# Four-layer gated block on one core: score products in adjacent pairs, value product in four column strips

## The chip, the core and the metric

The kernel runs on one NeuronCore of a Trainium2 chip as one launch. The metric is the device time of the launch in microseconds (us). The engines in it are TensorE (PE; its weight loads are listed apart as PEld), VectorE (DVE), ScalarE (ACT), GpSimd (POOL) and the queues that start transfers (SP, POOL).

## The reference

Four residual steps on x (4 batches, 512 tokens, 128 features). The change touches the third one, an attention with 16 heads of 8 features from 512 queries to 77 context rows per batch:

```python
x = x + tanh(g_xattn[0]) * xattn0(ctx, layernorm(x), W_b)            # step A: one head, 77 keys
x = x + tanh(g_ffn[0])   * ffn0(layernorm(x), ...)                    # step B: 8-bit quantised MLP
x = x + tanh(g_xattn[1]) * xattn1(layernorm(x), ctx, ctx, mask, ...)  # step C
x = x + tanh(g_ffn[1])   * moe(layernorm(x), wqkv, w1, w2)            # step D: top 2 of 8 experts

# xattn1
Q = split(query @ W_q.T); K = split(key @ W_k.T); V = split(value @ W_v.T)   # (b, 16, s, 8)
scores = einsum('bhqd,bhkd->bhqk', Q, K) / sqrt(8)
scores = where(mask, -inf, scores)
attn_w = nan_to_num(softmax(scores))
out = einsum('bhqk,bhkd->bhqd', attn_w, V)
return merge(out) @ W_o.T
```

## The kernel before

The program is written with one instruction stream for each engine and semaphores between them; nothing reorders it. Steps A and B come first, then step C with the router of step D woven in, then the scattering of rows to experts, the expert loop over 39 tiles, and the gathering of the result.

**Step C.** A batch b has 4 token tiles of 128 tokens (TB) and 8 score units (UNITS): unit u is token tile u // 2 and half u % 2 of the heads. A head group is four heads (HG), which lie in 32 of the 128 feature rows, and its scores have 4 x 77 = 308 columns (GC). `scores(b, u)` makes two head groups: for each a bf16 product of the identity with the mask values (`mneg`, L629), and on top of it in the same PSUM bank an fp32 product of 32 rows of `qT` with the same 32 rows of `kblk` (L630). On DVE `softmax(b, u)` takes the maximum (L991) and subtracts it (L994); on ACT `expC` takes the exponential (L419) into `pC` (tile name `space`). DVE's `sums` (L1000) adds each head's row. The two halves of `wide` are buffers for units, so unit n waits for the subtraction of unit n - 2.

The 16 heads' 1232 score columns are then cut into key blocks (HCH), here 10 (NCH): nine of 128 columns and one of 80. For each, PE transposes four 128-token pieces (`turn_p`, L651) into bank 2 or 3, ACT copies the result to one of two buffers of `pTC` (`copy_pT`, L427), and PE multiplies with `vblk` (`pv`, L663): `vblk` holds the values of the block's keys, each head's in its own 8 of 128 output columns and zeros elsewhere. All ten products add up in bank 1.

**The order of work in step C.** A hand-written loop of NCH slots n for each batch b sets the order on every engine: PE does `turn_p(b, n)`, `scores(b + 1, n)` while n < 8, and `pv(b, n - 1)`; then come pieces at fixed slots: `turn_r` (L677) and `spread_r` (L682) spread the reciprocals of the row sums in slots 0 and 1, `wo(b - 1)` (L692) is in slot 2, and the router of step D for batch b - 1 has its steps 0, 1, 2 in slots 5, 6, 9. DVE's step 1 of the router is one long run of small instructions (L1033 to L1063); its end releases PE's step 2 (L713, L714). DVE's `softmax(b + 1, 7)` stands behind this run, ACT's `expC(b + 1, 7)` behind that, and ACT's `copy_pT(b, 8)` behind the exponential. `attn_out(b)` (L1016) on DVE ends a batch. Before the first batch's loop, units 2 to 7 of batch 0 run by themselves (unit 0 and 1 a little earlier).

## Time and profile before

| | |
|---|---|
| median of three runs | 472.52 us (469.72 to 472.85) |
| span of the profiled execution, first to last instruction | 471.6 us |
| busy in it: PE, DVE, ACT, POOL | 339.0, 260.9, 140.6, 96.5 us |
| stretch of step C (first score unit to last value product) | 121.3 to 315 us |
| mean granted TensorE clock over the span | 0.764 of full speed |

The profiled execution's time outside its span isn't listed with it; its span lies 0.9 us under the median of the runs and within their spread, so differences in the span are read as differences in the time. Starts are in us from the first instruction. The listed end of a matmul is modelled and overlaps with the next one's start, so a matmul's cost is read from its start to the next one's start.

### The profile page before, as it was taken

What the parts mean: (1) busy time and instruction counts of PE and PEld (TensorE: products, weight loads), DVE (VectorE), ACT (ScalarE), POOL (GpSimd) and SP (SyncE); (2) the same over time, 40 slices, a digit from 0 to 9 for tenths busy, and PEclk for the clock granted to TensorE, in tenths of its full rate; (3) what the DMA queues carried; (4) which work ended last, traced back from release to release, by engine and by line L of the source; (5) the groups of instructions that cost most, each with busy time, mean ns of one, the idle gap of its engine ahead of it and who ended that gap; (6) DMA issues with size and microseconds to landing.
All of it is one profiled execution on the core that took longest, in us unless ns stands there. A gap on an engine that the chain in (4) does not pass through costs nothing.

```text
span 471.6 us, 5266 instructions
## 1 busy us (share of the span) xinstructions
PE 339.0 (72%) x1327; PEld 198.6 (42%) x1329; DVE 260.9 (55%) x753; ACT 140.6 (30%) x310; POOL 96.5 (20%) x156
## 2 busy tenths in 40 slices
PE   1157645545899899999789996862019999999930
PEld 0157521132333434444343553532006777777720
DVE  4748986997336513759862786475702333333314
ACT  1021025452141222333322243311013545455510
POOL 8400000017100000000033002414321334334430
PEclk9999955565555555999955897985557999999975
DMA  8991013900000000000000000101011111111127
GB/s 248 328 330 28 2 8 70 303 0 1 2 0 0 0 1 0 0 1 0 0 18 30 0 0 12 37 11 35 24 47 30 54 44 55 51 52 51 39 58 217
DMA packets 30192, 25.79 MB, mean 55 GB/s; under 512 B 8362, under 2 KB 26273, under 8 KB 30171
## 3 DMA queue, kind: packets, MB, share of 16 engines
q1 hardware_dynamic: 26011, 12.56, 10.2%
q0 software_dynamic: 4160, 12.99, 8.1%
q8 instruction: 9, 0.15, 0.1%
q14 instruction: 12, 0.10, 0.1%
HBM read 11.35 MB, written 14.49 MB: 55 GB/s over the span
## 4 chain that ended last, share of the span: by engine, by line
PE 56%; DVE 26%; issue 7%; DMA 4%; POOL 4%; ACT 2%; SPq 1%; POOLq 0%; DVEq 0%; ACTq 0%
PE wide L630 12%; PE bank L663 7%; PE wide L756 6%; PE bank L771 5%; PE wide L757 5%; PE bank L651 3%; PE wide L629 3%; PE bank L764 3%; DVE st L814 2%; DVE amh L965 2%; DVE h L843 2%; DVE space L961 2%; DMA space<-expert_out 2%; DVE rv L830 1%; POOL expert_rows L339 1%
## 5 line engine op out<-in xcount | busy, mean ns | idle before, releaser
L339 POOL DMA_INDIRECT expert_rows<-pay,slot x32 | 30.8, 964 | 194.8 <-DVE slot L1082 186.3
L630 PE MATMUL wide<-kblk,h2T 32*128 32x308 f32 x128 | 69.5, 633 | 0.0
L663 PE MATMUL bank<-pTC,vblk 128*128 128x512 f32 (+1 forms) x80 | 53.3, 758 | 10.6 <-ACT pTC L427 10.6
L991 DVE TENSOR_REDUCE mC<-wide 128x8 f32<-128x616 f32 x32 | 25.5, 798 | 60.3 <-PE wide L630 60.0
L348 POOL DMA_INDIRECT expert_out<-space x39 | 38.3, 982 | 70.7 <-DVE space L1137 70.7
L1131 DVE TENSOR_TENSOR space<-space,wide 128x352 f32<-128x352 f32 x39 | 20.3, 521 | 58.6 <-PE wide L757 55.9
L419 ACT ACTIVATE space<-space 128x616 f32<-128x616 f32 x32 | 22.8, 716 | 91.3 <-DVE space L994 91.3
L756 PE MATMUL wide<-w_s,space 128*128 x78 | 32.5, 499 | 3.7 <-issue 2.9
L515 PE MATMUL bank<-ident,h 128*128 128x128 f32 x48 | 13.3, 432 | 29.8 <-DVE h L843 29.0
L771 PE MATMUL bank<-w_s,space 128*128 (+1 forms) x234 | 32.8, 276 | 1.0 <-DVE space L1137 1.0
L651 PEld LDWEIGHTS bank<-ident,space 128*128 128x128 f32 (+1 forms) x160 | 23.6, 166 | 22.9 <-issue 18.6
L630 PEld LDWEIGHTS wide<-kblk,h2T 32*128 32x128 f32 x128 | 25.4, 246 | 18.1 <-issue 15.8
L651 PE MATMUL bank<-ident,space 128*128 128x128 f32 (+1 forms) x160 | 29.9, 319 | 2.5 <-ACT space L419 2.5
L757 PE MATMUL wide<-w_s,space 128*128 x78 | 30.7, 476 | 0.0
L771 PEld LDWEIGHTS bank<-w_s,space 128*128 128x128 f32 (+1 forms) x234 | 29.2, 191 | 1.5 <-issue 1.4
L427 ACT ACTIVATE pTC<-bank 128x512 f32<-128x512 f32 (+1 forms) x40 | 23.1, 587 | 20.9 <-PE bank L651 20.9
L476 ACT ACTIVATE space<-wide 128x352 f32<-128x352 f32 x39 | 18.1, 463 | 33.2 <-PE wide L756 33.2
L994 DVE TENSOR_TENSOR space<-wide,mC 128x616 f32<-128x616 f32 x32 | 25.6, 799 | 1.1
L1137 DVE TENSOR_SCALAR space<-bank,space 128x128 f32<-128x128 f32 x39 | 13.7, 351 | 21.9 <-PE bank L771 21.9
L629 PE MATMUL wide<-mneg,identb 128*128 128x308 bf16 x64 | 24.2, 378 | 0.0
L663 PEld LDWEIGHTS bank<-pTC,vblk 128*128 128x128 f32 (+1 forms) x80 | 14.3, 223 | 23.3 <-ACT pTC L427 12.7
L515 PEld LDWEIGHTS bank<-ident,h 128*128 128x128 f32 x48 | 8.6, 217 | 37.0 <-DVE h L843 36.1
(209 smaller groups left out, 512.2 us busy)
## 6 DMA issues: line engine op xcount, KB each, us to landing
expert_rows<-blank POOLq DMA_DIRECT2D x2, 2970.0 KB, 19.2
w_s<-in_w1T SPq DMA_DIRECT2D x1, 2816.0 KB, 10.0
expert_rows<-blank POOLq DMA_DIRECT2D x1, 2574.0 KB, 29.8
space<-expert_rows SPq DMA_DIRECT2D x39, 66.0 KB, 1.8
space<-expert_out SPq DMA_DIRECT2D x8, 256.0 KB, 3.1
xs<-in_x SPq DMA_DIRECT2D x4, 256.0 KB, 5.1
w_s<-in_w2T SPq DMA_DIRECT2D x2, 512.0 KB, 11.9
out<-xs SPq DMA_DIRECT2D x4, 256.0 KB, 3.3
```

The source lines that it names most:

```text
L339: pool.indirect_dma_start(tbl, bass.IndirectOffsetOnAxis(ap=slot[:, k, t:t + 1], axis=0), pay[:, b % 2, k, j, :], None).then_inc(rows_sent ...
L348: pool.indirect_dma_start(planes, bass.IndirectOffsetOnAxis(ap=mpay[:, j, D:D + 1].bitcast(I32), axis=0), my[:, j, :], None, bounds_check= ...
L427: act.activation(pTC[0:w, q % 2, :], bank[2 + q % 2][0:w, :], ACT.Copy).then_inc(pTC_ready, 1)
L629: pe.matmul(o, identb[:], mneg[:, j, None, :].broadcast_to([P, HG, KS]), start=True, stop=False)
L630: ins = pe.matmul(o, qT[r, b, j * P:(j + 1) * P], kblk[r, :, b * KS:(b + 1) * KS], start=False, stop=True)
L651: ins = pe.transpose(bank[2 + q % 2][0:w, j * P:(j + 1) * P], pC[:, (b * TB + j) % (2 * TB), c0:c0 + w], ident[:])
L663: pe.matmul(bank[1][:], vblk[0:w, c, b, :], pTC[0:w, q % 2, :], start=(c == 0), stop=(c == NCH - 1)).then_inc(pv_done, 1)
L756: pe.matmul(wide[:, 2 * p, 0:F], mhT[:, p, :], w1_s[:, bass.ds(e * 2 * F, F)]).then_inc(e_gate, 1)
L757: pe.matmul(wide[:, 2 * p + 1, 0:F], mhT[:, p, :], w1_s[:, bass.ds(e * 2 * F + F, F)]).then_inc(e_w1, 1)
L771: ins = pe.matmul(bank[1][:, p * P:(p + 1) * P], mhidT[0:n, p, c, :], w2_s[0:n, bass.ds(e * NF * D + c * D, D)], start=(c == 0), stop=(c = ...
L991: link(dve.tensor_reduce(m.rearrange("p (g l) -> p g l", g=2), s, AX.X, ALU.max))
L994: dve.tensor_tensor(pC[:, t % (2 * TB), (u % 2) * HU:(u % 2 + 1) * HU].rearrange("p (g l k) -> p g l k", g=2, l=HG), s, m.rearrange("p (g ...
```

## The change

The key blocks follow the head groups: each of the 4 head groups (308 columns) is cut in thirds of 103, 103 and 102 columns, 12 blocks in all, and the block list runs over the four groups first and then over the thirds. A block's keys belong to one head group, so its product fills only 32 output columns. `pv(b, t)` now does the t-th third of all four groups as four products, each to its own 32 partitions of bank 1, from blocks 4t to 4t + 3; it stands in slot 7 (t = 0), in slot 11 (t = 1) and behind the loop (t = 2). `pTC` has 8 buffers, and `vblk` has 32 output columns for a block. `scores` issues both mask products and then both score products. The loop has 12 slots; `sums_end` on DVE moves from slot 9 to slot 11, behind the router's step 2.

```diff
-    HCH = [(c * P, min(P, HK - c * P)) for c in range((HK + P - 1) // P)]
+    THIRD = (GC + 2) // 3
+    HCH = [(g * GC + t * THIRD, min(THIRD, GC - t * THIRD)) for t in range(3) for g in range(NG)]
...
-        va = sb("va", [KS, NB, D]); vblk = sb("vblk", [P, NCH, NB, D])
+        va = sb("va", [KS, NB, D]); vblk = sb("vblk", [P, NCH, NB, HG * DH])
...
-        pTC = sb("pTC", [P, 2, S])
+        pTC = sb("pTC", [P, 2 * NG, S])
...
-                if q >= 2:
-                    act.wait_ge(pv_done, q - 1)
+                if q >= 2 * NG:
+                    act.wait_ge(pv_done, q - 2 * NG + 1)
...
+                o = [wide[:, 2 * (n % 2) + i, 0:GC].rearrange("p (l k) -> p l k", l=HG) for i in range(2)]
                 for i in range(2):
-                    g = 2 * (u % 2) + i
-                    r = slice(32 * g, 32 * g + 32)
-                    o = wide[:, 2 * (n % 2) + i, 0:GC].rearrange("p (l k) -> p l k", l=HG)
-                    pe.matmul(o, identb[:], mneg[:, j, None, :].broadcast_to([P, HG, KS]), start=True, stop=False)
-                    ins = pe.matmul(o, qT[r, b, j * P:(j + 1) * P], kblk[r, :, b * KS:(b + 1) * KS], start=False, stop=True)
+                    pe.matmul(o[i], identb[:], mneg[:, j, None, :].broadcast_to([P, HG, KS]), start=True, stop=False)
+                for i in range(2):
+                    r = slice(32 * (2 * (u % 2) + i), 32 * (2 * (u % 2) + i) + 32)
+                    ins = pe.matmul(o[i], qT[r, b, j * P:(j + 1) * P], kblk[r, :, b * KS:(b + 1) * KS], start=False, stop=True)
                 ins.then_inc(sC_psum, 1)
...
-            def pv(b, c):
-                q, w = NCH * b + c, HCH[c][1]
-                pe.wait_ge(pTC_ready, q + 1)
+            def pv(b, t):
+                q = NCH * b + NG * t
+                pe.wait_ge(pTC_ready, q + NG)
...
-                pe.matmul(bank[1][:], vblk[0:w, c, b, :], pTC[0:w, q % 2, :],
-                          start=(c == 0), stop=(c == NCH - 1)).then_inc(pv_done, 1)
+                for g in range(NG):
+                    c = NG * t + g
+                    w = HCH[c][1]
+                    pe.matmul(bank[1][32 * g:32 * g + 32, :], vblk[0:w, c, b, :], pTC[0:w, (q + g) % (2 * NG), :],
+                              start=(t == 0), stop=(t == 2)).then_inc(pv_done, 1)
...
-                    if n >= 1:
-                        pv(b, n - 1)
+                    if n % NG == NG - 1 and n > NG:
+                        pv(b, n // NG - 1)
...
-                pv(b, NCH - 1)
+                pv(b, NCH // NG - 1)
...
-                        if n % 2 and n > 1:
+                        if n % 2 and 1 < n < 2 * TB + 2:
                             sums(b + 1, n // 2 - 1)
```

On PE, at the end of the second batch's loop from slot 7's unit on, the work stands so before (L651 is four transposes of a key block, L629 and L630 a mask and a score product, L663 a value product, L713 and L714 the router's step 2; a row counts products, and an fp32 product is two instructions in the trace):

```order
L629 MATMUL wide<-mneg,identb 128x308
L630 MATMUL wide<-kblk,h2T 128x308
L629 MATMUL wide<-mneg,identb 128x308
L630 MATMUL wide<-kblk,h2T 128x308
L663 MATMUL bank<-pTC,vblk 128x512
L651 MATMUL bank<-ident,space 128x128 x4
L663 MATMUL bank<-pTC,vblk 128x512
L651 MATMUL bank<-ident,space 80x128 x4
L663 MATMUL bank<-pTC,vblk 128x512
L713 MATMUL bank<-ohs,before 128x32
L714 MATMUL bank<-priorb,onesb 128x32
L663 MATMUL bank<-pTC,vblk 128x512
```

And after, from slot 7 (four transposes, a unit, four strips) over the router's step 2 (L718, L719) to the batch's last value products:

```order
L653 MATMUL bank<-ident,space 103x128 x4
L629 MATMUL wide<-mneg,identb 128x308 x2
L632 MATMUL wide<-kblk,h2T 128x308 x2
L668 MATMUL bank<-pTC,vblk 32x512 x4
L653 MATMUL bank<-ident,space 102x128 x8
L718 MATMUL bank<-ohs,before 128x32
L719 MATMUL bank<-priorb,onesb 128x32
L653 MATMUL bank<-ident,space 102x128 x8
L668 MATMUL bank<-pTC,vblk 32x512 x8
```

The mask products stand together and the score products stand together; the value products have left the slots 1 to 6, and two thirds of them come behind the router's step 2, where before one of ten did.

On DVE, at the same place (L1062 and L1063 end the router's step 1, L991 to L1000 are the unit 7 and its sums, L1007 and L1009 the reciprocals, L1067 the first of step 2), before:

```order
L1063 CAST ohs<-qkm 128x32
L991 TENSOR_REDUCE mC<-wide 128x8
L994 TENSOR_TENSOR space<-wide,mC 128x616
L1000 TENSOR_REDUCE sC<-space 128x16 x2
L1007 RECIPROCAL rC<-sC 128x64
L1009 TENSOR_TENSOR rC<-rC,rowany 128x64
L1067 TENSOR_SCALAR gp<-ge 128x4
```

And after:

```order
L1068 CAST ohs<-qkm 128x32
L996 TENSOR_REDUCE mC<-wide 128x8
L999 TENSOR_TENSOR space<-wide,mC 128x616
L1005 TENSOR_REDUCE sC<-space 128x16 x2
L1072 TENSOR_SCALAR gp<-ge 128x4
```

The unit 7 stays right behind the router's step 1, and the reciprocals move behind step 2.

## Rows read from the trace of the kernel before

**Rows 1.** The page: busy time, and the span in 40 slices (busy tenths, granted clock tenths).

```profile
PE 339.0 (72%) x1327; PEld 198.6 (42%) x1329; DVE 260.9 (55%) x753; ACT 140.6 (30%) x310; POOL 96.5 (20%) x156
...
PE   1157645545899899999789996862019999999930
...
DVE  4748986997336513759862786475702333333314
...
PEclk9999955565555555999955897985557999999975
```

**Rows 2.** The chain that ended last, by engine.

```profile
PE 56%; DVE 26%; issue 7%; DMA 4%; POOL 4%; ACT 2%; SPq 1%; POOLq 0%; DVEq 0%; ACTq 0%
```

**Rows 3.** Busy time by stretch of step C: PE, PEld, DVE, ACT, POOL, granted clock.

```profile
121.30:154.60 33.30, 30.14 (x55) 10.79 (x54) 16.64 (x21) 8.69 (x12) 0.00 (x0) 0.50 0.00 0
154.60:187.90 33.30, 33.30 (x70) 14.38 (x71) 11.99 (x15) 7.89 (x13) 0.00 (x0) 0.50 0.00 0
187.90:200.90 13.00, 12.83 (x46) 6.00 (x47) 9.26 (x10) 4.34 (x8) 0.00 (x0) 1.00 0.00 0
200.90:235.60 34.70, 31.21 (x131) 15.75 (x129) 26.86 (x77) 11.50 (x20) 0.00 (x0) 1.00 0.00 0
235.60:240.80 5.20, 3.79 (x6) 1.46 (x7) 4.96 (x16) 1.77 (x4) 0.00 (x0) 0.50 0.00 2
240.80:263.00 22.20, 22.20 (x54) 10.66 (x52) 6.42 (x10) 4.89 (x8) 7.86 (x8) 0.50 0.07 25
263.00:286.80 23.80, 19.13 (x79) 9.71 (x77) 21.73 (x69) 8.00 (x15) 0.00 (x0) 1.00 0.00 0
290.70:315.00 24.30, 19.37 (x89) 11.50 (x87) 13.27 (x71) 8.54 (x16) 7.65 (x8) 0.92 0.08 24
```

**Rows 4.** The page's groups of instructions: value products.

```profile
L663 PE MATMUL bank<-pTC,vblk 128*128 128x512 f32 (+1 forms) x80 | 53.3, 758 | 10.6 <-ACT pTC L427 10.6
```

**Rows 5.** PE in order of time, clock at full speed: a unit between two transposes.

```profile
201.29 0.30 PE L629 MATMUL wide<-mneg,identb 128*128 128x308 bf16 x1
201.52 0.78 PE L630 MATMUL wide<-kblk,h2T 32*128 32x308 f32 x2
202.23 0.31 PE L629 MATMUL wide<-mneg,identb 128*128 128x308 bf16 x1
...
203.18 0.60 PE L677 MATMUL bank<-ident,rC 128*16 128x128 f32 x4
203.62 0.60 PE L651 MATMUL bank<-ident,space 128*128 128x128 f32 x4
```

**Rows 6.** PE in order of time, clock at half speed, third batch's loop.

```profile
245.90 1.06 PE L651 MATMUL bank<-ident,space 128*128 128x128 f32 x4
246.75 0.47 PE L629 MATMUL wide<-mneg,identb 128*128 128x308 bf16 x1
247.14 1.39 PE L630 MATMUL wide<-kblk,h2T 32*128 32x308 f32 x2
248.46 0.44 PE L629 MATMUL wide<-mneg,identb 128*128 128x308 bf16 x1
...
250.15 2.08 PE L663 MATMUL bank<-pTC,vblk 128*128 128x512 f32 x2
252.16 2.07 PE L682 MATMUL bank<-rT,spread 16*128 16x512 f32 x2
```

**Rows 7.** PE in order of time, end of the second batch's loop.

```profile
230.80 1.02 PE L663 MATMUL bank<-pTC,vblk 128*128 128x512 f32 x2
231.66 0.60 PE L651 MATMUL bank<-ident,space 128*80 128x128 f32 x4
237.01 2.08 PE L663 MATMUL bank<-pTC,vblk 128*128 128x512 f32 x2 [4.74 <-ACT pTC L427]
```

**Rows 8.** ACT in order of time, end of the second batch's loop.

```profile
235.75 0.72 ACT L419 ACTIVATE space<-space 128x616 f32<-128x616 f32 x1 [5.96 <-DVE space L994]
236.37 1.06 ACT L427 ACTIVATE pTC<-bank 128x512 f32<-128x512 f32 x2
```

More of the change, by code:

```diff
@@ L229, in _ @@
                     a, z = max(c0, hd * KS), min(c0 + n, (hd + 1) * KS)
-                    cols = slice(hd * DH, (hd + 1) * DH)
-                    sp.dma_start(vblk[a - c0:z - c0, c, :, cols], va[a - hd * KS:z - hd * KS, :, cols]).then_inc(vblk_ready, 16)
+                    l = hd % HG
+                    sp.dma_start(vblk[a - c0:z - c0, c, :, l * DH:(l + 1) * DH],
+                                 va[a - hd * KS:z - hd * KS, :, hd * DH:(hd + 1) * DH]).then_inc(vblk_ready, 16)
             sp.dma_start(w1_s[:].rearrange("p (e f) -> p e f", e=E), w1T.rearrange("e d f -> d e f")).then_inc(ld_exp, 16)
@@ L423, in copy_pT @@
                 act.wait_ge(pTC_psum, q + 1)
-                if q >= 2:
-                    act.wait_ge(pv_done, q - 1)
+                if q >= 2 * NG:
+                    act.wait_ge(pv_done, q - 2 * NG + 1)
                 w = HCH[c][1]
-                act.activation(pTC[0:w, q % 2, :], bank[2 + q % 2][0:w, :], ACT.Copy).then_inc(pTC_ready, 1)
+                act.activation(pTC[0:w, q % (2 * NG), :], bank[2 + q % 2][0:w, :], ACT.Copy).then_inc(pTC_ready, 1)
             def copy_rT(b):
@@ L660, in pv @@
                     pe.wait_ge(vblk_ready, 16 * sum(z - a + 1 for a, z in HEADS))
-                if c == 0 and b >= 1:
+                if t == 0 and b >= 1:
                     pe.wait_ge(oT_ready, b)
-                pe.matmul(bank[1][:], vblk[0:w, c, b, :], pTC[0:w, q % 2, :],
-                          start=(c == 0), stop=(c == NCH - 1)).then_inc(pv_done, 1)
+                for g in range(NG):
[3 more added lines that the diff above has]
+                              start=(t == 0), stop=(t == 2)).then_inc(pv_done, 1)
             def turn_r(b):
```

## The prediction

> **What bounds the kernel now.** I first read the page's totals and the chain. PE is busy for 339.0 of 471.6 us [rows 1], and it holds 56% of the chain that ended last, with DVE at 26% [rows 2]. An average doesn't say what the change is worth, so I cut step C, which alone is touched, into stretches [rows 3]. The reader should look at three columns of each row: PE busy, DVE busy, granted clock.
>
> [...] In the second batch's loop (200.9 to 235.6) PE is busy for 31.2 and DVE for 26.9 of 34.7 us: both are close to the bound. That batch ends with a wait of 4.74 us on PE [rows 7]. It is put down to ACT, but ACT itself had been waiting 5.96 us for DVE [rows 8]: its copy stands behind the exponential of unit 7, which stands behind DVE's long router step. The clock falls to 0.50 just there, and stays until 263.0 in the third batch [rows 3]. The last batch (290.7 to 315.0) has no scores, and DVE's router runs in a row with PE's short pieces.
>
> So the stage has three kinds of stretch: PE-bound at half clock, DVE-bound at full clock, and batch ends at which value products queue behind DVE's router. The change helps the first, can't help the second, and lengthens the third.
>
> **Score units.** A value product of 512 columns behind work of its own kind takes 230.80 to 231.66, 0.86 us for its two instructions, so 0.43 each at full clock [rows 7] (80 instructions for 40 products [rows 4]). By columns, a score instruction of 308 streams for 0.26 (half clock: 0.52), and a bf16 mask product, a quarter of an fp32 one, for 0.13 (0.26). A score product however takes 201.52 to 202.23, 0.71 instead of 0.52: 0.19 goes to the change from full-height work to 32 rows and back. At half clock it is 247.14 to 248.46, 1.32 instead of 1.04: 0.28. A unit takes 1.89 us [rows 5] and 3.40 us (246.75 to 250.15) [rows 6].
>
> After the change a unit has one entry to and one exit from the 32-row form. If nothing runs side by side it costs, at full clock, 0.13 + 0.23 (second mask product with the entry) + 4 x 0.26 + 0.19 = 1.59; at half clock 0.26 + 0.39 + 4 x 0.52 + 0.28 = 3.0. That saves 0.3 and 0.4 and needs no new property of the array.
>
> If products on different rows run side by side, I take this form: an fp32 product's second instruction uses the same array rows as its first and must follow it, and instructions start in program order, so only the first product's second instruction meets the second product's first. Four rounds become three: 1.33 and 2.48 us, a saving of 0.56 and 0.92. No row of this trace has two such products side by side: the bounds are 0.4 (none) and 1.43 (two rounds) at half clock, and I take 0.92, by the order of the instructions.
>
> **Value products.** Ten of 0.86 to 0.97 us become twelve strips. Each strip streams the same 512 columns: 0.43 us an instruction at full clock, 0.86 at half. Four strips have 8 instructions: one after the other 3.4 (6.9) us, in the paired form 5 rounds, 2.15 (4.3) us, all four side by side 2 rounds, 0.86 (1.7) us. With 0.1 (0.2) for entry I take 2.25 (4.5) a group, 6.75 (13.5) a batch, where ten products take about 9.3 (18.5). The narrow form itself seems free to leave: the 16-column transposes at 203.18 pass to the 128-column ones at 203.62, four in 0.44, as four of the others take [rows 5].
>
> Two more blocks a batch mean eight more transposes, 0.86 (1.7) us by 245.90 to 246.75 for four at half clock [rows 6], and two more copies on ACT (1.06 for two [rows 8]), which has room: 11.5 of 34.7 us busy [rows 3]. The eight `pTC` buffers let the copies run ahead. The block copies into `vblk` and its smaller clearing lie far before their first use: nothing.
>
> [...]
>
> **The sum, stretch by stretch.**
> - 121.3 to 154.6, eight units of batch 0 at half clock: 8 x 0.92 = -7.3.
> - First batch's loop, now 46.3 us, 33.3 of them at half clock. After, at half clock: eight slots of transposes and unit, 8 x (0.91 + 2.48) = 27.1; reciprocals 0.86 + 2.0 (252.16 to 254.16 in the same loop one batch later [rows 6]), 2.9; one group of strips 4.5; then 16 transposes in a row, 3.4. That is 37.9. In this dense run I expect the clock to rise, as it did before a little after dense stretches of full-array products (188, 263 us). The last two groups then take 4.5: 42.4, -3.9. At half clock they take 9.0: 46.9, +0.6.
> - Second batch's loop, now 39.9. DVE's unit 7 ends 34.8 us into it. DVE was idle for 7.8 of these, some 3.4 of it for PE, which goes: 31.4. Then 1.3 for ACT's exponential and copy; only then the last 8 transposes and two groups: 5.4 at full, 10.7 at half clock, where now two products stand. 38.1 to 43.4; I take 41, +1.1.
> - Third batch's loop, now 49.9, because 22.2 of it are PE-bound at half clock [rows 3]. As the second if the clock is up, 41; if it stays at half, seven slots 23.7, reciprocals 2.9, `wo` and router pieces 4.2, then 9.6 for slots 7 to 9, 0.4, 1.7 and 9.0: 51.5. I take 44, -5.9.
> - Last batch: DVE's router sets the pace, and behind its step 1 stand 8 transposes and two groups, 5.4, where 1.7 was: +4 (+9 at half clock).
>
> -7.3 - 3.9 + 1.1 - 5.9 + 4 = -12: 471.6 becomes 460. Paired overlap alone spans 450 (clock up throughout) to 470.
>
> **Rivals.**
> 1. *The clock stays low (slower).* Now value products keep every slot dense in full-array work; the clock rose at 187.9 and 263.0 out of such runs. It didn't rise from 121.3 to 154.6, with PE busy for 30.1 of 33.3 us [rows 3] mostly in 32-row products. After the change slots 0 to 6 are like that stretch, and of strips of 32 columns no row tells what they do to the clock. PE will also wait more at full clock, and the fall at 235.6 came out of a wait of 4.74 us. If PE isn't at full clock from the second batch's loop on, that loop is PE-bound like the third, 51.5 (+11.6), with -7.3, +0.6, +1.6 and +9: +15.5, 487. It decides once PE spends the second loop at 0.50. Its cases lie between 471 and 487; I take 480.
> 2. *Nothing runs side by side (slower).* Units save 0.3 to 0.4, groups cost 3.5 (7.1). Stretch by stretch -3.2; +5.6 to +12.6; +0.9 to +8.7; -9.1 to +10; +6.4 to +14.2: from +0.6 to +42; middle +18, 490. [...]
> 3. *Full overlap.* Units of 1.97 at half clock and two-round strips: -11.4, about -12, -3, -11, +2: -35, 436. Against it: a product's two instructions share its strip.
> 4. *DVE takes it all back (no change).* The batch ends eat what the first 33 us give: 468 to 476.
>
> **How the numbers follow.** Forecast 0.38 (450 to 469), rival 1 0.24, rival 2 0.20, rival 3 0.10, rival 4 0.08. A difference of 1% (4.7 us) is about what a measurement of this kernel tells from none. Faster: 0.36 + 0.10 = 0.46; slower: 0.21 + 0.17 + a part of rival 4, 0.41; same 0.13. From 446 to 492 lie all of the forecast, of rivals 1 and 4 and over half of rival 2: 0.82.
>
> **What would show it.** In the new profile: a unit of 2.5 us at half clock (3.0 if serial, 2.0 if full overlap); a group of strips in 2.25 (4.5) against 3.5 (7.1) us; the first transposes of a key block at about 147 instead of 154.6; the clock rising near 184; the second batch's last strips some 7 to 12 us behind the exponential of unit 7. Wrong would make me a clock at 0.50 through the second and third loop, or strips that take 3.4 us at full clock.

## The result and the profile after

| | before | after |
|---|---|---|
| median of the runs | 472.69 us (469.72 to 473.64) | 433.39 us (427.27 to 438.7) |
| span of the profiled execution | 471.6 us | 432.3 us |
| mean granted TensorE clock in it | 0.764 | 0.737 |
| ratio after to before | | 0.9139, 95% interval 0.9011 to 0.9268 |

The change makes the kernel 8.6% faster. The forecast was 460 us, and its range began at 446. The executions of a kernel fall into a faster and a slower group: the ratios here and below compare the faster ones, while the medians are of all runs, and some of the profiled executions, that of after among them, are slower ones.

The page of the profile after, the same lines as [rows 1] and [rows 2]: busy time, the span in 40 slices, and the chain by engine.

```profile
PE 291.3 (67%) x1375; PEld 183.6 (42%) x1377; DVE 257.8 (60%) x753; ACT 144.3 (33%) x318; POOL 93.5 (22%) x156
...
PE   1357734734797988987998467720099999999910
...
DVE  5648995987649796689588855457023343333314
...
PEclk9999955556555798555857595555589999999975
...
PE 44%; DVE 35%; issue 8%; POOL 4%; DMA 4%; ACT 3%; SPq 1%; POOLq 0%; DVEq 0%; ACTq 0%
```

PE has 48 more instructions and is busy 47.7 us less, at a lower mean clock. DVE's share of the chain has grown from 26% to 35%.

The windows of the kernel after, cut at what each stage begins with (columns as in [rows 3]: stretch, length, then busy time of PE, PEld, DVE, ACT, POOL, then the granted clock): units 0 to 7 of batch 0 up to the first transpose of a key block, then the four batches' loops.

```profile
118.30:141.20 22.90, 18.80 (x55) 6.47 (x53) 16.16 (x21) 8.69 (x12) 0.00 (x0) 0.50 0.00 0
141.20:167.90 26.70, 23.71 (x127) 11.87 (x127) 21.23 (x26) 12.84 (x22) 0.00 (x0) 0.83 0.00 1
167.90:208.60 40.70, 35.26 (x152) 19.56 (x148) 31.75 (x91) 14.47 (x26) 0.84 (x1) 0.58 0.00 1
208.60:249.20 40.60, 31.77 (x153) 17.35 (x149) 31.64 (x91) 14.47 (x26) 8.67 (x10) 0.66 0.05 16
249.20:276.90 27.70, 19.94 (x105) 12.36 (x101) 13.87 (x70) 9.51 (x18) 9.51 (x11) 0.68 0.08 25
```

Cut the same way, every kernel of this study gives a line of the next table. "Front" is all that lies ahead of the first score unit, "rest" all behind the last batch's loop; in brackets the us of a stage at half clock. It is worked out from one profiled execution of each kernel, and such an execution lies up to about 10 us off the median of its kernel. So the table shows where time sits, and only the ratios say how much a kernel wins.

| us | front | units | loop 1 | loop 2 | loop 3 | loop 4 | rest | span |
|---|---|---|---|---|---|---|---|---|
| before | 121.3 | 33.3 (33.3) | 46.3 (33.2) | 40.0 (5.2) | 49.9 (26.0) | 25.1 (4.6) | 155.8 | 471.6 |
| after | 118.3 | 22.9 (22.9) | 26.6 (9.0) | 40.8 (34.1) | 40.5 (27.3) | 27.7 (17.5) | 155.4 | 432.3 |
| difference | -3.0 | -10.4 | -19.7 | +0.8 | -9.4 | +2.6 | -0.4 | -39.3 |
| forecast | 0 | -7.3 | -3.9 | +1.1 | -5.9 | +4 | 0 | -12 |

The units and every loop have the sign that was forecast for them, but the first loop is far off, the units and the third loop are short by 3 us each, and the front was not forecast at all.

**The score pair.** PE in order of time, first at half clock (to be held against [rows 6], where one score product takes 1.32), then at full clock (against [rows 5], 0.71 for one):

```profile
118.30 0.72 PE L629 MATMUL wide<-mneg,identb 128*128 128x308 bf16 x2
118.95 1.40 PE L632 MATMUL wide<-kblk,h2T 32*128 32x308 f32 x4
120.28 0.69 PE L629 MATMUL wide<-mneg,identb 128*128 128x308 bf16 x2
...
148.78 0.44 PE L629 MATMUL wide<-mneg,identb 128*128 128x308 bf16 x2
149.15 0.79 PE L632 MATMUL wide<-kblk,h2T 32*128 32x308 f32 x4
149.87 0.69 PE L653 MATMUL bank<-ident,space 128*103 128x128 f32 x4
```

The four instructions of the pair (x4) take from 118.95 to 120.28, 1.33 us, and from 149.15 to 149.87, 0.72. That is the time of one product, so two rounds, not the three of the forecast. Their single starts in the trace, which the merged row hides, are 118.95, 118.96, 119.63 and 119.64: two begin together, and 0.67 us later the other two. A unit costs 1.98 us at half clock (118.30 to 120.28), where it cost 3.40.

**The strips.** The same view around the first group of four value products, at full clock, and of one at half clock:

```profile
159.00 1.06 PE L668 MATMUL bank<-pTC,vblk 103*32 103x512 f32 x8
160.00 0.64 PE L653 MATMUL bank<-ident,space 128*102 128x128 f32 x4
...
196.49 1.94 PE L668 MATMUL bank<-pTC,vblk 103*32 103x512 f32 x8
198.36 1.95 PE L653 MATMUL bank<-ident,space 128*102 128x128 f32 x8
```

Eight instructions take 1.00 us, and 1.87 at half clock. A single value product of before took 0.86 us at full clock in [rows 7], and 0.97 where it followed a unit (229.40 to 230.37). So here too four products cost about as much as one; the forecast had 2.25 and 4.5. Four instructions start from 159.00 to 159.02, the other four from 159.45 to 159.47. In a row the eight would take 3.4 us, an estimate from the 0.43 us of an instruction in [rows 7].

**The end of the second loop.** PE and ACT there, the counterpart of [rows 7] and [rows 8]:

```profile
200.79 0.21 PE L718 MATMUL bank<-ohs,before 128*128 128x32 bf16 x1 [0.48 <-DVE ohs L1068]
200.84 0.19 PE L719 MATMUL bank<-priorb,onesb 128*128 128x32 bf16 x1
203.56 1.94 PE L653 MATMUL bank<-ident,space 128*102 128x128 f32 x8 [2.54 <-ACT pTC L429]
205.44 3.27 PE L668 MATMUL bank<-pTC,vblk 103*32 103x512 f32 x16
```

```profile
202.31 0.72 ACT L421 ACTIVATE space<-space 128x616 f32<-128x616 f32 x1 [5.96 <-DVE space L999]
202.93 1.06 ACT L429 ACTIVATE pTC<-bank 102x512 f32<-102x512 f32 x2
```

ACT waits the same 5.96 us for DVE. The exponential of unit 7 starts 34.4 us into the loop, where before it was 34.8, though PE's work has shrunk. Behind it now stand eight transposes and two groups of strips, up to 208.6: 6.3 us, of which 3.2 are the strips. So loop 2 gained nothing. In loop 4 the stretch from the router's step 2 to the end takes 6.46 us (270.42 to 276.88), where before it took 2.47 (313.32 to 315.79); step 2 itself comes 1.4 us earlier in the loop, which leaves the loss of 2.6.

**The front.** GpSimd and DVE in order of time in the first 17 us. Before:

```profile
9.56 4.38 POOL L306 MEMSET vblk<- 128x5120 f32 x1
...
14.89 1.85 POOL L312 MEMSET pay<- 128x2112 f32 x1
16.68 0.12 POOL L313 MEMSET prior<- 128x8 f32 x1
...
10.71 6.05 DVE L830 TENSOR_SCALAR rv<-mv 128x16 f32<-128x16 f32 x1
```

And after:

```profile
9.57 1.40 POOL L308 MEMSET vblk<- 128x1536 f32 x1
...
13.70 0.12 POOL L315 MEMSET prior<- 128x8 f32 x1
...
9.89 3.89 DVE L835 TENSOR_SCALAR rv<-mv 128x16 f32<-128x16 f32 x1
```

An instruction of 16 columns that reads nothing of GpSimd's takes 6.05 us and ends at 16.76, as GpSimd's run of instructions ends at 16.80. After, the run ends at 13.82 and the instruction at 13.78. Everything up to the first score unit then comes 3.0 us earlier. The forecast put the smaller clearing of `vblk` down at nothing, because its first use is far away; its price lay with an instruction that has nothing to do with it. Here the DVE instruction got in behind none of the instructions of this run of GpSimd's, only behind its last: it ended 0.04 us before the run did, in both kernels. Two experiments below add to this, one of them with an exception.

### The profile page after: what moved, and what is told of

It reads as the page before. It is cut to its first block, busy times and chain, and to the rows that moved or that the text cites. A ratio compares the mean times of both kernels' runs of the same rounds, so it can differ in the third digit from the quotient of the medians.

```text
span 432.3 us, 5371 instructions
## 1 busy us (share of the span) xinstructions
PE 291.3 (67%) x1375; PEld 183.6 (42%) x1377; DVE 257.8 (60%) x753; ACT 144.3 (33%) x318; POOL 93.5 (22%) x156
## 3 DMA queue, kind: packets, MB, share of 16 engines
q1 hardware_dynamic: 26031, 12.56, 11.2%
## 4 chain that ended last, share of the span: by engine, by line
PE 44%; DVE 35%; issue 8%; POOL 4%; DMA 4%; ACT 3%; SPq 1%; POOLq 0%; DVEq 0%; ACTq 0%
PE wide L761 7%; PE bank L776 6%; PE wide L762 5%; DVE space L999 4%; PE bank L653 4%; DVE mC L996 3%; PE wide L632 3%; PE bank L668 3%; PE bank L769 3%; DVE st L819 2%; DVE amh L970 2%; DVE h L848 2%; DVE space L966 2%; DVE sC L1005 2%; DMA space<-expert_out 2%
## 5 line engine op out<-in xcount | busy, mean ns | idle before, releaser
L350 POOL DMA_INDIRECT expert_out<-space x39 | 38.3, 981 | 69.8 <-DVE space L1142 69.8
L653 PE MATMUL bank<-ident,space 128*103 128x128 f32 (+1 forms) x192 | 40.9, 359 | 10.3 <-ACT pTC L429 7.4
L653 PEld LDWEIGHTS bank<-ident,space 128*103 128x103 f32 (+1 forms) x192 | 30.8, 205 | 30.3 <-ACT pTC L429 14.8
L632 PE MATMUL wide<-kblk,h2T 32*128 32x308 f32 x128 | 37.4, 674 | 0.0
L429 ACT ACTIVATE pTC<-bank 103x512 f32<-103x512 f32 (+1 forms) x48 | 27.8, 587 | 20.3 <-PE bank L653 20.3
L776 PE MATMUL bank<-w_s,space 128*128 (+1 forms) x234 | 32.8, 276 | 1.0 <-DVE space L1142 1.0
L478 ACT ACTIVATE space<-wide 128x352 f32<-128x352 f32 x39 | 18.1, 463 | 33.2 <-PE wide L761 33.2
L1005 DVE TENSOR_REDUCE sC<-space 128x16 f32<-128x1232 f32 x16 | 22.5, 1426 | 0.0
L362 ACT ACTIVATE hT<-bank 128x512 f32<-128x512 f32 x12 | 7.1, 594 | 45.5 <-PE bank L517 28.6
L752 PE MATMUL bank<-ident,space 128*128 128x128 f32 x39 | 11.0, 282 | 16.5 <-DMA space<-expert_rows 16.5
L629 PE MATMUL wide<-mneg,identb 128*128 128x308 bf16 x64 | 19.5, 400 | 1.5 <-DVE space L999 1.5
## 6 DMA issues: line engine op xcount, KB each, us to landing
w_s<-in_w1T SPq DMA_DIRECT2D x1, 2816.0 KB, 10.4
```

The source lines that it names most:

```text
L350: pool.indirect_dma_start(planes, bass.IndirectOffsetOnAxis(ap=mpay[:, j, D:D + 1].bitcast(I32), axis=0), my[:, j, :], None, bounds_check= ...
L429: act.activation(pTC[0:w, q % (2 * NG), :], bank[2 + q % 2][0:w, :], ACT.Copy).then_inc(pTC_ready, 1)
L632: ins = pe.matmul(o[i], qT[r, b, j * P:(j + 1) * P], kblk[r, :, b * KS:(b + 1) * KS], start=False, stop=True)
L653: ins = pe.transpose(bank[2 + q % 2][0:w, j * P:(j + 1) * P], pC[:, (b * TB + j) % (2 * TB), c0:c0 + w], ident[:])
L776: ins = pe.matmul(bank[1][:, p * P:(p + 1) * P], mhidT[0:n, p, c, :], w2_s[0:n, bass.ds(e * NF * D + c * D, D)], start=(c == 0), stop=(c = ...
L1005: dve.tensor_reduce(sC[:, j, :], pC[:, (b * TB + j) % (2 * TB), :].rearrange("p (h k) -> p h k", h=H), AX.X, ALU.add).then_inc(sums_done, 1)
```

## The experiments

The first two take the change apart: is the score pair the whole gain, or do the strips carry a part of their own? The next two ask what the front is worth. Stages are given in the order of the table, from the front to the rest.

**The score pair alone.** Before, with the two mask products first and the two score products behind them.

```diff
                 for i in range(2):
-                    pe.matmul(o, identb[:], mneg[...], start=True, stop=False)
-                    ins = pe.matmul(o, qT[r, b, ...], kblk[r, :, ...], start=False, stop=True)
+                    pe.matmul(o[i], identb[:], mneg[...], start=True, stop=False)
+                for i in range(2):
+                    ins = pe.matmul(o[i], qT[r, b, ...], kblk[r, :, ...], start=False, stop=True)
```

> The kernel before with the new order inside a score unit alone (both mask products, then both score products); ten value products as before. Theory A (two fp32 products on different array rows run side by side in full, so that a pair costs what one did): a unit at half clock takes about 1.95 us instead of 3.40, the eight units before the first batch's loop save about 10 us, the first loop about 10 more, the second and third little each, since DVE sets their pace: 472.7 becomes about 448. Theory B (only the fewer changes of array form count, the products follow each other): a unit takes 3.0 us at half clock, 465 to 469.

Measured: 432.63 us (428.89 to 435.42), ratio 0.9234 (0.9149 to 0.9318). Stages: 121.3 | 22.9 (22.9) | 26.9 (5.3) | 38.4 (8.8) | 37.8 (7.1) | 24.5 (1.2) | 155.3. Its windows of loops 2 and 3:

```profile
171.10:209.50 38.40, 30.50 (x137) 15.85 (x136) 31.93 (x92) 13.27 (x24) 0.00 (x0) 0.89 0.00 1
209.50:247.30 37.80, 29.79 (x137) 15.32 (x136) 31.61 (x92) 13.27 (x24) 7.86 (x8) 0.91 0.04 15
```

That is more than either theory expected (448, or 465 to 469). The interval overlaps that of the full change: moving two lines gives nearly all of it. Loops 2 and 3 are even shorter than after (38.4 and 37.8 against 40.8 and 40.5), with DVE busy for the same 31.6 to 31.9 us. Only the front is back at 121.3.

**The strips alone.** The change with the old order of mask and score products.

```diff
                 for i in range(2):
                     pe.matmul(o[i], identb[:], mneg[...], start=True, stop=False)
-                for i in range(2):
                     ins = pe.matmul(o[i], qT[r, b, ...], kblk[r, :, ...], start=False, stop=True)
```

> The changed kernel with the old order inside a score unit (mask, score, mask, score); strips, 12 blocks and their slots stay. Theory A (four strips side by side in two rounds): a group costs about 1.9 us at half clock and 1.0 at full, the first loop loses some 12 us of PE work, the eight units before it save nothing, and the front of the program keeps its 3 us: about 455. Theory B (the strips' gain comes from pairing in five rounds): a group 4.5 us at half clock, 465 to 470. If the two parts are independent, this saving and that of the run with the new unit order alone add up to the 39 us of the whole change; if they both relieve PE until DVE sets the pace, they add up to more.

Measured: 465.01 us (456.2 to 471.02) beside 468.43 for before. The four runs spread too far for an interval, so this is no measured gain. It lies in the range that was expected of the dearer strips (465 to 470), though the strips cost what the cheaper ones were to cost; 455 was expected of those. Stages: 118.3 | 33.3 (33.3) | 43.3 (40.0) | 42.3 (27.3) | 40.7 (23.9) | 27.5 (13.6) | 154.0, span 459.5. The units are at 33.3 again, and the first loop is PE-bound at a clock of 0.54.

**The old clearing back in the full change.** Three more clearings of `vblk` on GpSimd, each waiting for the one before, so that it clears as many columns as before did.

```diff
+            link(pool.memset(vblk[:], 0.0))
+            link(pool.memset(vblk[:], 0.0))
+            link(pool.memset(vblk[:, 0:4], 0.0))
```

> The changed kernel with vblk cleared three times and a third, so that GpSimd's clearing takes as long as in the kernel before (4.4 us instead of 1.4). Theory A (DVE's first step of the layer norm waits until GpSimd's run of clearings ends, so 3 us of the gain come from the smaller vblk): every start after 20 us is 3 us later, 3 us slower than the changed kernel. Theory B (the earlier start came from the arrival of x): no difference.

Measured: 431.57 us, ratio 0.9186 (0.9087 to 0.9284); first score unit at 118.8, 0.5 us later and not 3. GpSimd and DVE in order of time:

```profile
9.56 1.40 POOL L308 MEMSET vblk<- 128x1536 f32 x1
11.02 1.38 POOL L309 MEMSET vblk<- 128x1536 f32 x1
12.45 0.53 POOL L310 MEMSET vblk<- 128x512 f32 x1
...
9.88 1.11 DVE L838 TENSOR_SCALAR rv<-mv 128x16 f32<-128x16 f32 x1
11.03 1.40 DVE L839 TENSOR_SCALAR rstd<-rv 128x16 int32<-128x16 int32 x1
```

My expectation failed, and the rows say why. The first DVE instruction ends at 10.99, as the first memset ends at 10.96; the second ends at 12.43, as the second memset ends at 12.40. The waits between the four pieces let DVE in. DVE's next nine instructions, with two inputs each, take 0.17 to 0.18 us as ever, beside the third and fourth memset. But the fourth memset begins a run without a wait, and it holds DVE again, now at the step that applies the layer norm:

```profile
17.17 0.24 POOL L318 MEMSET prior<- 128x8 f32 x1
...
14.74 4.29 DVE L851 TENSOR_SCALAR h<-xs,mv,rstd 128x128 f32<-128x128 f32 x8
```

The first of these eight starts at 14.74 and ends at 17.31, as GpSimd's run ends at 17.41. All eight end at 19.03, against 18.56 after, where they were not held and took 2.26 us together. These 0.47 us are the 0.5 by which the first score unit is late. So the pieces did not make the clearing free: they let DVE do a chain of small work within it, and what was left of the run still held DVE. Which of DVE's instructions are held matters too: all that were are TENSOR_SCALAR.

**The clearing first, in the kernel before.** GpSimd's clearings and index tables moved ahead of its three transfers that blank the expert rows; nothing else changes.

```diff
-            for k in range(3):
-                ...
-                pool.dma_start(tbl_v[:, a:z, :], blank[...]).then_inc(tbl_blank, 16)
             pool.memset(vblk[:], 0.0).then_inc(vblk_zero, 1)
...
+            for k in range(3):
+                ...
+                pool.dma_start(tbl_v[:, a:z, :], blank[...]).then_inc(tbl_blank, 16)
```

> The kernel before with GpSimd's clearings and index patterns ahead of the three large blanking transfers that it starts, instead of behind them. Theory A (DVE waits for the clearings): they are over by about 13 us instead of 17, and the program gets 3 to 5 us shorter (about 468.5). Theory B (the clearing plays no part): no difference; the blanking itself ends long before its use either way.

Measured: 466.29 us (463.0 to 475.99), ratio 0.993 (0.9882 to 0.9978). Stages: 117.5 | 33.3 (33.3) | 40.5 (20.9) | 40.0 | 49.9 | 25.2 | 155.8. In the trace `vblk` is cleared from 5.48 to 9.84, GpSimd's run ends at 12.72, and the held DVE instruction takes 2.50 us, until 12.69. That shows the front's share by itself: 3.8 us in this profile, and 0.2 to 1.2% of the time by the interval. The rows also show an exception to what the front showed:

```profile
9.97 0.19 DVE L830 TENSOR_SCALAR rv<-mv 128x16 f32<-128x16 f32 x1
10.19 2.50 DVE L831 TENSOR_SCALAR rstd<-rv 128x16 int32<-128x16 int32 x1
```

The first of them is the one that took 6.05 us before. Here it starts as GpSimd is in its index tables (9.80 to 10.85) and isn't held; the next one is. So a run without a wait can let such an instruction in, and what decides stays open. The first loop is a surprise: the same PE work as before takes 40.5 instead of 46.3, since the clock rose after 20.9 instead of 33.2 us.

**Two score products on the same rows.** The full change, but both products of a pair read the same 32 rows. This changes what is computed: one of each two head groups gets the other's scores.

```diff
-                    r = slice(32 * (2 * (u % 2) + i), 32 * (2 * (u % 2) + i) + 32)
+                    r = slice(64 * (u % 2), 64 * (u % 2) + 32)
```

> The changed kernel with both score products of a unit on the same 32 array rows (the second head group of each half reads the first one's rows, so those scores, and what follows from them, are not the reference's; the work has the same shape). Order, instructions and array form are those of the changed kernel; only the side-by-side running is excluded. Theory A (the gain of a unit is the overlap): a unit at half clock takes 3.0 us, as the forecast priced a serial one, instead of 1.95, and the eight units before the first loop 30 us instead of 22.9; the time is about 455. Theory B (the gain comes from leaving out array-form changes): the unit stays near 1.95 us and the time at 433.

Measured: 459.39 us, ratio 0.9723 (0.9648 to 0.9798). Stages: 118.3 | 30.0 (30.0) | 39.7 (36.8) | 44.8 (37.4) | 43.5 (29.8) | 27.1 (11.2) | 154.1. PE in order of time, a unit, and then the place where the row sums are spread:

```profile
130.93 0.69 PE L629 MATMUL wide<-mneg,identb 128*128 128x308 bf16 x2
131.55 2.42 PE L632 MATMUL wide<-kblk,h2T 32*128 32x308 f32 x4
133.90 0.69 PE L629 MATMUL wide<-mneg,identb 128*128 128x308 bf16 x2
...
154.62 1.39 PE L632 MATMUL wide<-kblk,h2T 32*128 32x308 f32 x2
155.32 1.21 PE L687 MATMUL bank<-rT,spread 16*128 16x512 f32 x1
155.81 1.23 PE L632 MATMUL wide<-kblk,h2T 32*128 32x308 f32 x2
156.34 1.05 PE L687 MATMUL bank<-rT,spread 16*128 16x512 f32 x1
```

The pair takes 2.35 us (131.55 to 133.90) instead of 1.33 and the unit 2.97, which is the serial price of 3.0 that the prediction worked out. So of the units' 10.4 us, 3.3 come from standing next to each other (33.3 to 30.0) and 7.1 from the different rows (30.0 to 22.9); the ratio is 0.9723 against 0.9139 overall. The second piece also shows how. L687 comes behind both score products in the program and uses other rows. Its first instruction starts at 155.32, ahead of the second score product's at 155.81. So here instructions on rows that were free didn't wait for those queued ahead of them on busy rows. The forecast had assumed that they start in program order; this row speaks against it.

**The strips one behind the other.** The full change, but the four products of the second group lie in one strip of 32 columns, and those of the third in another; the first group is as it was. This changes what is computed: head groups are added into one another's columns. The amount of work is the same.

```diff
-                    pe.matmul(bank[1][32 * g:32 * g + 32, :], vblk[0:w, c, b, :], ...
+                    h0 = 32 * (g if t == 0 else t)
+                    pe.matmul(bank[1][h0:h0 + 32, :], vblk[0:w, c, b, :], ...
```

> The changed kernel with the second and third group of value products all sent to one column strip (the sums land in the wrong 32 rows, so the attention output is not the reference's; sizes and order are unchanged). Theory A (four strips run side by side): such a group takes 3.4 us at full clock and 6.9 at half instead of 1.0 and 1.9; two groups a batch stand behind the router's end, so the batches 2 to 4 get 5 to 10 us longer each, and the time is 450 to 465. Theory B (a strip product is cheap by itself since it loads only 32 columns): no difference.

Measured: 446.29 us (444.75 to 452.3), ratio 0.9474 (0.9417 to 0.9531), less than the 450 to 465 that were expected. Stages: 118.3 | 22.9 | 36.6 (31.4) | 43.0 (23.9) | 44.0 (27.3) | 31.3 (17.1) | 154.4. PE at the end of its second loop, the first four of sixteen instructions and what comes behind them all:

```profile
214.01 3.36 PE L669 MATMUL bank<-pTC,vblk 103*32 103x512 f32 x4
...
220.77 0.68 PE L653 MATMUL bank<-ident,space 128*103 128x128 f32 x4
```

The first four instructions, half of the second group, take 3.36 us, where after a whole group takes 1.87 at the same clock: 0.85 us each, the serial price of the prediction (0.86). The two groups together take 6.76 us, where after has 3.20, though the clock rises in the middle: a window up to 217.0 has a granted clock of 0.50, the one behind it 1.00. From 217.22 on, the third group, which lies in another strip, starts beside the rest of the second, ahead of instructions that stand before it in the program; so even here a part runs side by side. Products on different columns do run side by side, then, and it matters against strips in a row: +10.0, +2.2, +3.5 and +3.6 us in the four loops of the profile (the first with the clock at half for 31.4 us instead of 9.0). Strips in a row would lose against the ten plain products that the change replaced: 0.9474, where the score pair alone has 0.9234. Side by side they only make up for that.

**Ballast.** The full change with one idle product of 128 x 512 in slots 1 to 6 of loops 1 to 3, into the bank that the strips overwrite later. It adds PE work, 18 products, and no result, and in slot 1 of each loop the waits that its operands and its bank need.

```diff
+                    if 1 <= n < UNITS - 1 and b + 1 < NB:
+                        ballast(b, n)      # pe.matmul(bank[1][:], ident[:], w1_s[:, 0:S])
```

> The changed kernel with one idle product (identity times a weight tile, 128 x 512 fp32, into bank 1 before its first real use, result never read) in each of slots 1 to 6 of the first three batches: PE work of 0.86 us at full and 1.7 us at half clock, 18 times, where the kernel before had its value products. Theory A (with strips PE has so little to do in the slots that its clock falls to half speed in the second and third loop, and comes back late, which costs more than the work saved): the granted clock of the second and third loop stays near 1.0, and the time falls to 428 to 431 in spite of 15 to 30 us more of PE work. Theory B (the low clock there is chance, DVE sets the pace anyway): the time stays or rises by 3 to 10 us.

Measured: 430.38 us (429.07 to 440.02), ratio 0.9142 (0.9102 to 0.9183). Stages: 118.3 | 22.9 | 28.1 (5.4) | 38.8 (10.2) | 38.2 (6.8) | 27.7 (17.1) | 154.3. Its windows of loops 2 and 3:

```profile
169.30:208.10 38.80, 30.12 (x164) 15.31 (x160) 31.55 (x91) 14.47 (x26) 1.13 (x1) 0.87 0.00 1
208.10:246.30 38.20, 29.51 (x164) 15.30 (x160) 31.57 (x91) 14.47 (x26) 7.70 (x8) 0.91 0.04 15
```

With 12 more instructions a loop PE is busy for less time than after (30.12 against 35.26, 29.51 against 31.77), because the clock is at 0.87 and 0.91 instead of 0.58 and 0.66. The runs agree: the mean clock of the six is 0.764 to 0.795, that of after's four 0.728 to 0.765. Each loop is 2.0 or 2.3 us shorter in the profile. In the ratio this doesn't show. So the strips' price in loops 2 and 3 is in part a lower clock, as the first rival had it.

**The score pair with the clearing first.** The first and the fourth experiment together, no strips.

> The kernel before with the new order inside a score unit and with GpSimd's clearings ahead of its blanking transfers; no strips. The savings found apart (36 us and about 4 us at the front) should add up, since they lie in different stretches: about 429. If strips were worth something beside them, this kernel would be slower than the changed one (433); theory: it is faster by 3 to 5 us, since the strips' gain in the first loop is lost behind the router in the later ones.

Measured: 424.63 us (422.75 to 430.69), ratio 0.901 (0.8963 to 0.9056). Stages: 117.5 | 22.9 | 32.8 (17.8) | 38.3 (8.9) | 37.7 (7.0) | 24.2 (1.1) | 155.5. This is the best version of the study, some 9 us below the full change by the medians. The intervals of the two ratios overlap a little (0.9056 and 0.9011), so that it beats the full change isn't shown; against the ballast (0.9102 to 0.9183) and the full change with the old clearing (0.9087 to 0.9284) they don't overlap. The full change with the clearing first and nothing else was not run.

**Four attempts at the ends of the loops.** Since two thirds of the strips stand behind the router's step 2 and the exponential of unit 7, these kernels move both out of the loop: all key blocks first, then the router's step 2, then unit 7's exponential.

```diff
-                    if b + 1 < NB and n < UNITS:
+                    if b + 1 < NB and n < UNITS - 1:
                         expC(b + 1, n)
...
-                    if b >= 1 and n in ROUTER_SLOTS:
+                    if b >= 1 and n in ROUTER_SLOTS[:2]:
...
+                if b >= 1:
+                    router(b - 1, 2)
+                if b + 1 < NB:
+                    expC(b + 1, UNITS - 1)
```

The full change with this order and the second group of strips in slot 9:

> The changed kernel with the end of each batch put in another order: PE does its second group of strips in slot 9 and its third behind slot 11, and only then the router's step 2; ACT does its copies 8 to 11 before the exponential of unit 7. So no value product stands behind DVE's router step. Theory A (two groups and eight transposes behind the router cost each of the batches 2 to 4 some 3 to 5 us): batches 2 and 3 take 36 to 37 us instead of 40.7 and the last 25 instead of 27.7, the time is about 422. Theory B (DVE's own work sets the batches' length and what PE does at their ends is hidden): no difference from 433.

The same with the clearing first:

> The run v1_tail with GpSimd's clearings ahead of its blanking transfers as well. With vblk's small clearing the run of clearings ends near 9.5 us, before DVE's first step of the layer norm, so the start of the first score unit moves from 118.3 to about 114.5: some 4 us under v1_tail, 418. If nothing moves, the wait at the front had another cause in this kernel.

The order without strips, with the score pair and the clearing first:

> The kernel before with the new order inside a score unit, the clearings first, and the same reordering of the batch ends with its ten full products (products 8 and 9 before the router's step 2, ACT's copies before the exponential of unit 7). Two products of 0.9 us and one wait leave the batch ends: 1 to 2 us in each of batches 2 and 3, about 421, from 424.6 without the reordering. Beside v2_tail_clear_first this says what strips are worth once nothing stands behind the router: theory, within 1% of each other, since DVE sets the length of the batches.

And all of it, strips, order, clearing first and ballast:

> v2_tail_clear_first with the idle products of e7_ballast in slots 1 to 6. If the low clock still costs PE time in batches 2 and 3 there, this is 1 to 3 us faster (415 to 417) although PE does more; if DVE alone sets the pace once the tails are gone, it is the same or 1 us slower.

| | median, us | ratio (95%) | loop 1 | loop 2 | loop 3 | loop 4 |
|---|---|---|---|---|---|---|
| order, strips | 430.52 | 0.9159 (0.9069 to 0.9248) | 25.0 (5.1) | 37.5 (20.5) | 41.0 (27.3) | 30.0 (17.0) |
| and clearing first | 427.40 | 0.9101 (0.9017 to 0.9185) | 34.1 (31.4) | 37.5 | 41.0 | 29.9 |
| order, clearing first, no strips | 435.01 | 0.9193 (0.9063 to 0.9323) | 32.3 (17.5) | 33.6 (0.6) | 41.9 (21.4) | 31.1 (14.1) |
| all, with ballast | 434.07 | 0.9268 (0.9211 to 0.9325) | 28.4 (6.4) | 33.6 (1.1) | 42.5 (19.4) | 30.5 (17.0) |

They were expected at 422, 418, 421 and 415 to 417 us, and none beats the score pair with the clearing first (0.901). In this set the runs of before spread from 466 to 480 us, so these four ratios are the least sure. In the second kernel the first score unit starts at 115.7 and not at 114.5: the clearings are over at 9.73, but a DVE instruction of 16 columns is held again, from 9.73 to 11.09, beside GpSimd's start of a transfer (9.68 to 11.12). Loop 2 does what was hoped: 33.6 us against 38.3, with the clock up. Loops 3 and 4 give it all back. PE and then DVE of the third kernel, at the head of its third loop:

```profile
205.13 1.12 PE L655 MATMUL bank<-ident,space 128*128 128x128 f32 x4 [2.07 <-ACT space L419]
...
209.07 1.01 PE L681 MATMUL bank<-ident,rC 128*16 128x128 f32 x4 [0.99 <-DVE pos L1081]
...
214.71 2.07 PE L686 MATMUL bank<-rT,spread 16*128 16x512 f32 x2
...
219.72 0.80 DVE L997 TENSOR_REDUCE mC<-wide 128x8 f32<-128x616 f32 x1 [5.26 <-issue]
...
223.42 0.75 DVE L1026 SCALAR_TENSOR_TENSOR xs<-bank,th,xs 128x512 f32<-128x512 f32 x1 [2.07 <-PE bank L696]
```

The pause has moved from the end of the loop to the head of the next. PE waits 2.07 us for unit 7's exponential, whose result the first transposes now need, and another 0.99 for DVE. Those rows are at half clock (transposes of 1.12 instead of 0.60), and so are the spreading of the row sums (2.07) and the units between, while DVE stands for 5.26 and 2.07 us with nothing to do. The 5.26 us are listed as "issue", but the score products that DVE needs start only at 218.27. DVE can't recover this: its 31.54 us of work in this loop then end at 41.9. This is read from the trace of one kernel; no run took the head's wait away again, so as a cause it is argued.

## Why the prediction was wrong, point by point

- **Half clock and PE-bound from 121.3 to 187.9, so that a us off PE is a us off the kernel.** Right. PE was busy for 63.4 of these 66.6 us at a granted clock of 0.50, DVE for 28.6 [rows 3]. The units fell by 10.4 us in eight units, 1.3 each, and a unit's PE work by 1.42.
- **The step that failed: "an fp32 product's second instruction uses the same array rows as its first and must follow it, and instructions start in program order, so only the first product's second instruction meets the second product's first."** The first half holds: in the pair at half clock a product's two starts are 0.67 us apart, and four instructions on the same rows start 0.51 to 0.68 us one behind the other. The second half was my assumption, and the runs speak against it. Instructions on free rows start ahead of queued ones on busy rows (the experiment with both on the same rows: 155.32 ahead of 155.81), and in the pair itself the instructions start two and two (118.95, 118.96, then 119.63, 119.64). So two products take two rounds: 1.33 us, not the 1.84 of three (3 x 0.52 + 0.28). The same step priced a group of strips at 2.25 (4.5) us where it costs 1.00 (1.87). It had named the bounds, 0.4 to 1.43 us saved for a unit; it measured 1.42, and I had given this end 0.10.
- **The serial price of a unit, 3.0 us.** Right: 2.97. The prices it was added up from also hold, each read from one start to the next. A score instruction behind one of its kind takes 0.26 us at full and 0.51 at half clock (189.32 to 189.58 and 132.22 to 132.74, both products on the same rows). A mask product with another behind it takes 0.14 and 0.26 (148.78 to 148.92 and 118.30 to 118.56, after), about a quarter of the 0.52 and 1.03 of two score instructions; the one that stands before the 32-row products takes 0.23 and 0.39 (148.92 to 149.15 and 118.56 to 118.95). What a score product takes beyond its two instructions, 0.19 and 0.28 in the forecast, comes once for two in a row: 2.35 us for four instructions of 0.51 at half clock.
- **The first loop, -3.9.** The largest error, 15.8 us, and most of it is the step above. The forecast's sum for a loop at half clock throughout was 46.9. With the measured prices, 1.98 for 2.48 in eight units and 1.87 for 4.5 in three groups of strips, the same sum is 35.0. One of the later kernels, the full change in the other order with the clearing first, has the same PE instructions in this loop and was at half clock for 31.4 us of it: 34.1 us. So at about the clock of before (33.2 of 46.3 us at half) some 12 us are work. Another 7.5 go with the clock (34.1 to 26.6), which was at half for 9.0 us only. I had expected it to rise near 184; in the trace after, full-clock rows stand from 147. Without strips it is alike: the score pair alone takes 26.9 us with 5.3 at half, and with the clearing first 32.8 with 17.8. Loop 1 is at half clock for anything from 5.1 to 40.0 us in these kernels, and for 20.9 or 33.2 in two with the same PE instructions (before, with and without the clearing first). What sets the moment of the rise isn't settled here; between those two it makes 5.8 us. How much of the 39 us it makes in another execution isn't known.
- **Second loop, +1.1.** +0.8, but this is luck: two misses cancel. I had DVE gain 3.4 us, the exponential of unit 7 coming 31.4 us into the loop, and some 9.6 us behind it. It came at 34.4, and 6.3 us stand behind it. That DVE's side bounds the loop and that the strips queue behind the exponential was right. Rival 1 also happened: the clock is at half for 34.1 of 40.8 us. It didn't make the loop 51.5 us long because PE's work was far less than I counted.
- **Third loop, -5.9.** It was -9.4: the loop comes down to the length of the second, though it is at half clock for 27.3 of 40.5 us, for which I had 51.5 (41 with the clock up, and I took 44). The two-round prices are why.
- **Last loop, +4.** +2.6. The place was right, and the stretch behind the router grew by 4.0 us (2.47 to 6.46). But +4 was the sum for full clock and five-round groups; measured was half clock, for which I had +9, and two-round groups, 3.6 us for both. These two cancel. The other 1.4 us are the router's step 2, which comes earlier.
- **The clearing of `vblk` at nothing.** Wrong by 3.0 us. I looked for its first use and not for what runs beside it.
- **Value products as part of the gain.** Not shown. The score pair alone has 0.9234 and the full change 0.9139, with overlapping intervals, and of the 4.5 us that lie between these ratios 3.0 are the front, which the strips shorten by having less to clear. In loop 1 they save 1.9 us at an equal time at half clock (25.0 us with 5.1 at half in the first of the last four kernels, 26.9 with 5.3 for the score pair alone). In loops 2 to 4 they lose 2.4, 2.7 and 3.2 us against plain products (after against the score pair alone). The ballast gives back 2.0 and 2.3 of the first two, and nothing of the last.
- **Rival 3, "full overlap", 436 us, had the right mechanism and nearly the right time.** I set it at 0.10 on one argument about program order, for which no row spoke.

## What to carry to other kernels

Where products of few rows stand between full-height ones, put those on different rows next to each other before anything else is tried: here one swapped loop gave 7.7% at no cost. Then ask what sets the pace afterwards; four column strips in the time of one brought nothing that the ratios show, in loops where DVE's side had become the bound and the strips stood behind its longest run. And look at what every small clearing runs beside, not only at who reads its result.

## What the runs showed of the hardware

- Two fp32 products of 32 rows on different rows take as long as one: 1.33 against 1.32 us at half clock. Four of 32 columns take 1.00 (1.87) us, where one full one took 0.86 to 0.97.
- A product on free rows overtakes one that is ahead of it in the program on busy rows (155.32 and 155.81).
- Less work for PE can mean a lower clock: 0.58 and 0.66 in loops with strips, 0.87 and 0.91 in the same loops with idle products added, 0.89 and 0.91 with plain products.
- A DVE instruction of 16 columns took 6.05 us beside a run of GpSimd instructions without a wait, 3.89 beside a shorter one, 2.50 where the run began earlier, 1.11 where waits cut it into pieces, and 1.36 beside the start of a transfer on GpSimd (9.73 to 11.09). It ended each time with GpSimd's run, piece or start, within 0.04 us. In one kernel the same kind of instruction passed in the middle of a run, in 0.19 us; instructions with two inputs took their usual 0.17 to 0.18 us beside the clearing.
